# First edge of each receiver block: a one-hot row pick on TensorE in place of an indirect row gather, with the own products moved into block 0

## The reference, cut to what matters

```python
h = node_features @ W + b_W;  xi, xj = split(h, 2)
xji = xj[senders] + (edge_features @ W_e + b_We)
xji = xji / (in_degree[receivers][..., None] + 1e-06)
nodes = xi + segment_sum(xji, receivers)             # layer 0
x = layernorm(x + nodes)
h = x @ W;  norm = dinv[src] * dinv[dst]             # layer 1, with self loops
out = segment_sum(h[src] * norm[:, None], dst) + b   # then batch norm, leaky relu
x = layernorm(x + leaky(batchnorm(out)))
```

## Time and profile before

| what | before |
|---|---|
| median of 3 runs | 942.07 us |
| runs | 942.12, 940.08, 942.07 us |
| span of the profiled execution, all that is given of its own time | 940.7 us |
| busy in the span: TensorE (PE), VectorE (DVE), ScalarE (ACT), GpSimd (POOL) | 890.2, 695.5, 454.9, 419.3 us |
| bytes moved | 244.8 MB |

### The profile page before, as it was taken

How to read it: one execution, slowest core, us unless ns; L and a number is a source line. 1 busy time by engine, 2 the same in 40 slices (tenths; PEclk the granted TensorE clock), 3 DMA queues, 4 the chain that set the end, 5 groups by cost and what they waited for, 6 DMA issues and landing times.

```text
span 940.7 us, 30861 instructions
## 1 busy us (share of the span) xinstructions
PE 890.2 (95%) x12193; PEld 794.2 (84%) x12193; DVE 695.5 (74%) x1636; ACT 454.9 (48%) x962; POOL 419.3 (45%) x498
## 2 busy tenths in 40 slices
PE   5679999999999999999999999999999999999995
PEld 4667888888988998989999999999988888888864
DVE  5898999999999998898888899888842111112255
ACT  3765665566656665565565556565542000000035
POOL 3347557555764555655565575544332011111100
PEclk9689999999999999999999999999999999999998
DMA  5475888899797987777687777688767887779635
GB/s 164 132 232 212 314 289 293 313 325 315 263 324 286 316 304 236 266 218 248 244 284 249 236 250 211 243 281 258 231 207 305 341 346 285 270 259 324 248 123 165
DMA packets 95727, 244.82 MB, mean 260 GB/s; under 512 B 41194, under 2 KB 63400, under 8 KB 89688
## 3 DMA queue, kind: packets, MB, share of 16 engines
q1 hardware_dynamic: 92312, 237.49, 72.5%
q0 software_dynamic: 2400, 4.88, 1.6%
q10 hardware_dynamic: 864, 0.39, 0.2%
HBM read 183.88 MB, written 58.85 MB: 258 GB/s over the span
## 4 chain that ended last, share of the span: by engine, by line
PE 81%; DVE 10%; issue 3%; ACT 2%; DMA 2%; POOL 0%; ACTq 0%; DVEq 0%
PE x_ps L846 24%; PE pair_ps L911 17%; PE pair_ps L828 13%; PE e_ps L865 10%; PE x_ps L854 9%; DVE key_oh L597 3%; DVE lo_oh L594 3%; PE j_ps L893 2%; DMA early_in<-sums_z 1%; PE pair_ps L920 1%; PE j_ps L894 1%; PE u_vps L1379 1%; ACT counts L1035 1%; DMA xsplit<-in_dst 1%; PE j_ps L943 1%
## 5 line engine op out<-in xcount | busy, mean ns | idle before, releaser
L1035 ACT CAST counts<-pair_ps 128x784 bf16<-128x784 f32 x391 | 315.4, 817 | 256.1 <-PE pair_ps L828 255.3
L846 PE MATMUL x_ps<-counts,xsplit 128*128 128x256 bf16 (+1 forms) x2450 | 306.1, 271 | 1.2 <-issue 1.2
L594 DVE TENSOR_TENSOR lo_oh<-counter,lo_t 128x1024 bf16<-128x1024 bf16 x391 | 274.4, 702 | 41.7 <-PE pair_ps L828 39.8
L846 PEld LDWEIGHTS x_ps<-counts,xsplit 128*128 128x128 f16 x2450 | 221.1, 98 | 31.4 <-issue 9.8
L597 DVE TENSOR_TENSOR key_oh<-counter,key_t 128x800 bf16<-128x800 bf16 x391 | 232.7, 595 | 0.0
L828 PE MATMUL pair_ps<-key_oh,lo_oh 128*128 128x100 bf16 x3128 | 208.5, 209 | 12.9 <-DVE key_oh L597 7.2
L828 PEld LDWEIGHTS pair_ps<-key_oh,lo_oh 128*128 128x128 bf16 x3128 | 182.9, 98 | 27.9 <-DVE key_oh L597 10.9
L865 PE MATMUL e_ps<-streams 128*32 128x128 f32 x3528 | 106.6, 274 | 0.0
L854 PE MATMUL x_ps<-counts,zown 128*128 128x256 bf16 (+1 forms) x840 | 105.9, 269 | 0.6 <-issue 0.6
L911 PE MATMUL pair_ps<-streams,zown 128*128 128x256 bf16 x878 | 99.0, 273 | 0.0
L865 PEld LDWEIGHTS e_ps<-streams 128*32 128x32 f32 x3528 | 93.4, 110 | 4.8 <-issue 1.0
(11 more groups left out here) (179 smaller groups left out, 881.1 us busy)
## 6 DMA issues: line engine op xcount, KB each, us to landing
streams<-in_edge_attr SPq DMA_DIRECT2D x196, 576.0 KB
counts_kept<-counts SPq DMA_DIRECT2D x10, 1600.0 KB, 9.2
streams<-counts_kept SPq DMA_DIRECT2D x6, 1600.0 KB, 6.5
counts<-counts_kept SPq DMA_DIRECT2D x4, 1600.0 KB, 6.5
counts_kept<-counts SPq DMA_DIRECT2D x2, 3136.0 KB, 12.1
streams<-counts_kept SPq DMA_DIRECT2D x2, 3136.0 KB, 14.6
edst<-in_dst SPq DMA_DIRECT2D x196, 4.5 KB, 1.9
counts<-in_x SPq DMA_DIRECT2D x3, 1024.0 KB, 8.9
```

The costliest lines, as they stand in the source:

```text
L594: dv.tensor_tensor(lo_oh[:, at % RING, :, :, :], counter[:, :, :].unsqueeze(1).to_broadcast([P, SW // 2, P, 2]), pairs(lo_t[b % 2][:, w]). ...
L846: last = nc.tensor.matmul(x_ps[:, 0, 0:n], xsplit[:, q // 2, q % 2, :], by_hi[:, q // 2, :], start=(q == 0), stop=(q == 2 * HS - 1))
L1035: a.copy(out.rearrange("p h (g n) -> p h g n", g=2), pair_ps[at % 2][:, :, 0:4 * KW].rearrange("p g (n h) -> p h g n", h=HI)[:, 0:HS]).the ...
```

## The change

The heads and the row gathers are gone. For each block SP (ScalarE's queue for blocks 1 to 3) loads 128 consecutive rows of `dst`, one a partition, with the next row's head as a 126th word (`load_rows`; four buffers, and one buffer with two loads for the last two blocks). ScalarE makes them float and subtracts the block's first receiver (`float_rows`). VectorE compares the row's head and the next row's head with each pair's threshold, in two operations (`find_below`, `pick_rows`), which gives a one-hot matrix of 128 rows by 128 pairs. TensorE multiplies that by the rows (`find_rows`), so that each pair gets its row, and VectorE counts in it (`count_row`, `start_of`), from PSUM. GpSimd has no part in it any more. For blocks 4 to 24 the steps for block b + 3 stand in block b: `float_rows` in slot 0 on ScalarE, `find_below` in slot 1 and `pick_rows` in slot 2 on VectorE, `find_rows` in slot 3 on TensorE, `count_row` in slot 8.

All 13 own products stand in slots 0 to 12 of block 0, each with the next piece's transposition behind it, in one PSUM buffer. x is loaded into the upper part of `streams`, where block 0's second group of edges comes later, so that group's load and its one-hots wait for the split of x. The reductions `largest` move into slots 0, 2 and 4 of block 0, `split_high` to slots 13 to 15 of block 0, `split_low` to slot 15 and to slots 2 and 4 of block 1. The far heads and their three spreads fall away.

```diff
-HIGH_AT, LOW_AT, HEADS_AT = (4, 6, 9), (7, 10, 13), (9, 11, 13)
+LARGEST_AT = (0, 2, 4)
+TOP_AT, SCALES_AT, SPREAD_AT = 5, 8, 12
+HIGH_AT, LOW_AT = (13, 14, 15), (15, 18, 20)
...
+        def load_rows(engine, b):
+            reach(engine, S["rows_float"], b - ROW_RING + 1)
+            engine.dma_start(rows_i[b % ROW_RING][:, :],
+                             bass.AP(tensor=dst.tensor, offset=first_row(b) * HR, ap=[[HR, P], [1, HR + 1]]))\
+                  .then_inc(rows_in[b % ROW_RING], 16)
...
             def load_edges(b, g, starts):
                 reach(sp, S["e_summed"], edge_group(b - 1, g) + 1)
+                if b == 0 and g == 1:
+                    sp.wait_ge(S["x_low"], len(X_PIECES))
+                    sp.wait_ge(S["x_turned"], len(OWN))
...
             for b in range(NB + 2):
                 u = b - 2
+                if b + ROW_RING < LATE:
+                    load_rows(sp, b + ROW_RING)
+                if b + ROW_RING == LATE:
+                    load_late_rows(sp)
...
-            def row_of(b):
-                pool.wait_ge(S["heads_counted"], b + 1)
...
-                gather(rows[b % 2][:, :], flat_dst, row_i[:, b:b + 1], row_in[b % 2])
...
-            def count_heads(b):
...
+            def find_below(b):
+                dve.wait_ge(S["rows_float"], b + 1)
+                reach(dve, S["picked"], b)
+                dv.tensor_scalar(below[:, :], even[:, :], rows[b % 2][:, 0:1], None, ALU.is_gt).then_inc(S["below"], 1)
+
+            def pick_rows(b):
+                dve.wait_ge(S["below"], b + 1)
+                reach(dve, S["found"], b - 1)
+                dv.scalar_tensor_tensor(out=pick[b % 2][:, :], in0=even[:, :], scalar=rows[b % 2][:, HR:HR + 1],
+                                        in1=below[:, :], op0=ALU.is_le, op1=ALU.mult).then_inc(S["picked"], 1)
...
-                    if s == 1 and b + 3 < NB:
-                        count_heads(b + 3)
+                    if s == 1 and 1 <= b < NB - 3:
+                        find_below(b + 3)
+                    if s == 2 and 1 <= b < NB - 3:
+                        pick_rows(b + 3)
                     if s == 2 and b + 1 < NB:
                         make_keys(b + 1)
...
+            def find_rows(b):
+                pe.wait_ge(S["picked"], b + 1)
+                if b >= 4:
+                    pe.wait_ge(S["tabled"], b - 2)
+                    pe.wait_ge(S["starts_known"], b)
+                nc.tensor.matmul(row_ps(b), pick[b % 2][:, :], rows[b % 2][:, :], start=True, stop=True)\
+                  .then_inc(S["found"], 1)
...
+                        if s < len(OWN):
+                            own_product(s)
+                        if s + 1 < len(OWN):
+                            turn_x(s + 1)
...
+                    if s == 3 and 1 <= b < NB - 3:
+                        find_rows(b + 3)
                     if s == 3 and b + 1 < NB:
                         turn_keys(b + 1)
-                    if b == 1 and s in HEADS_AT:
-                        spread_far_heads(HEADS_AT.index(s))
...
+            def float_rows(b):
+                if b < LATE:
+                    act.wait_ge(rows_in[b % ROW_RING], 16 * (b // ROW_RING + 1))
+                else:
+                    act.wait_ge(S["late_rows_in"], 32)
+                reach(act, S["found"], b - 1)
+                a.activation(rows[b % 2][:, 0:HR + 1], (rows_i[b % ROW_RING] if b < LATE else late_rows_i)[:, :],
+                             ACT.Identity, bias=shift[:, b:b + 1]).then_inc(S["rows_float"], 1)
...
                     if b < NB and s < slots(b):
                         pair_out(b, s)
...
+                    if s == 0 and 1 <= b < NB - 3:
+                        float_rows(b + 3)
```

More of the change, by code:

```diff
@@ L44 @@
 R = E // HR
-HEAD_SPAN, HEAD_MARGIN = 98, 16
+ROW_MARGIN = 31
+ROW_RING = 4
 PER = 7
@@ L108, in edge_group, with first_row @@
     return 2 * b + g
[L111 to L119, removed]
+def first_row(b):
+    return max(0, min(b * BN * E // (N * HR) - ROW_MARGIN, R - P))
+LATE = min(b for b in range(NB) if first_row(b) == R - P)
+assert all(first_row(b) + P < R for b in range(LATE))
 def early(k):
@@ L495, in check_edges @@
                 pool.sem_inc(S["e_checked"], 1)
-            for b in range(2):
-                row_of(b)
             windows(0)
-            row_of(2)
             windows(1)
             pad_degrees(0)
-            row_of(3)
             shares(0)
             for b in range(NB):
-                if 1 <= b < NB - 3:
-                    row_of(b + 3)
                 if b + 1 < NB:
@@ L702, in z_low @@
                 last.then_inc(S["z_low"], 1)
-            dve.wait_ge(S["heads_in"], 16)
-            dv.tensor_copy(heads[:, :], heads_i[:, :]).then_inc(S["heads_float"], 1)
             dve.wait_ge(S["consts"], 4)
-            dv.tensor_copy(th[:, :], th_i[:, :])
-            dv.tensor_copy(iota[:, :], iota_i[:, :])
-            dv.memset(total[:, :], 0.0)
-            step(dv.tensor_copy(ebase[:, :], ebase_i[:, :]))
-            dve.wait_ge(S["heads_broadcast"], 1)
-            step(dv.tensor_copy(heads_sb[:, 0:NEAR], heads_ps))
-            for b in range(3):
-                count_heads(b)
+            dv.tensor_copy(shift[:, :], shift_i[:, :]).then_inc(S["rows_ready"], 1)
+            step(dv.tensor_copy(iota[:, :], iota_i[:, :]))
+            dv.tensor_scalar(even[:, :], iota[:, :], 2.0, None, ALU.mult)
+            for i in range(2):
+                dv.tensor_copy(rows[i][:, HR + 1:HR + 2], base_i[:, :])
+            step(dv.tensor_copy(th[:, :], th_i[:, :]))
+            for b in range(2):
+                find_below(b)
+                pick_rows(b)
             step(dv.tensor_copy(counter[:, :, :], iota[:, :].unsqueeze(2).to_broadcast([P, P, 2])))
-            ready_own_weights()
-            largest(0)
-            largest(1)
             for b in range(2):
@@ L721, in _ @@
                 start_of(b)
-            largest(2)
+                find_below(b + 2)
+                pick_rows(b + 2)
+            dve.wait_ge(S["consts"], CONSTS)
+            dv.memset(total[:, :], 0.0)
+            step(dv.tensor_copy(ebase[:, :], ebase_i[:, :]))
+            for b in range(2, 4):
+                count_row(b)
+                start_of(b)
+            ready_own_weights()
             make_keys(0)
```

212 lines of the change are left out of this document (91 added, 121 removed).

## The result

The changed kernel takes **1040.31 us** (median of 6 runs, 1037.51 to 1045.77), the kernel before 942.1 beside it: a ratio of **1.1035 [1.1005, 1.1066]**. The forecast was 1029, with a range of 995 to 1055. The profiled execution has a span of 1038.4 us, so 97.7 of span were lost.

The account below looks back on a forecast made before the run. TensorE was taken to bound the steady blocks, with VectorE's lead as what the change touches. Span 940.7 - 1 (start) + 70 (stall) + 18 (clock) = 1027.7 us, plus 1.4 to the median: 1029 us, range 995 to 1055.

Parts of the forecast that it names:

- The mechanism: Slot 1, blocks 2 to 21: `find_below` waits for `float_rows` behind ScalarE's copy of slot 0; VectorE's lead goes, 3.5 us a block.
- some 4: Sign of being right: VectorE idle some 4 us ahead of `find_below` in each block from 2 to 21.
- some 65 us and more: Sign of being right: TensorE idle ahead of its counts of slots 3 and 4, some 65 us and more in all.
- The stall, +70: Blocks 2 to 21: TensorE waits for late one-hots, 20 blocks by 3.5 us, +70 us, ends 64 and 78.
- `find_rows`, costed at 0: TensorE's added product, 0.27 us a block, 5.4 us over 20 blocks if nothing hid it; taken as 0.
- The start, -1: Start to end of block 1: slot 0 starts 9 us sooner, largely given back; -1 us, ends -9 and +8.
- its end of +8: Upper end of the start's term: TensorE at half clock through the own products, or block 0's second edge group late.
- The clock, +18: Blocks 2 to 21: the new waits lower TensorE's clock in two blocks of three, 1.4 us each; ends 0 and 28.
- The rival whose time came nearest, 1039: Stall and clock fall in every block: 1038 plus 1.4, so 1039 us, up to 1055; chance 0.22.
- the lower ends: Low end of the rival with the stall but a clock that holds: 1011 us, down to 1000; chance 0.17.
- the upper ones: High end of the rival with stall and clock fall in every block: 1039 us, up to 1055; chance 0.22.
- Faster: Rival: the ring of four buffers covers the wait, decided in slot 1 of each block; 933 us, chance 0.07.

Follow-up runs that it names:

- e1: Against the changed kernel, `float_rows` issued in slot 10, one block sooner, work and data unchanged: 954.19 us, ratio 1.0117.
- e2: Against the kernel before, one wait added on VectorE in slot 1 of blocks 2 to 21 for ScalarE's copy of slot 0: 1013.67 us, ratio 1.0764.
- e4: Against e1, on SP the load of block 0's second group of edges stands behind the store of block 0's counts: 950.43 us, ratio 1.008.
- e6: Against e4, rows and one-hot in bf16 instead of f32 for the product that finds the row: 949.2 us.
- e10: Against a 952.39 us kernel with early splits of x, VectorE's halves moved from slots 6, 8, 10 of block 0 to 10, 12, 14: 940.5 us.
- e5: Against e4, start reordered: two reductions ahead of the first keys, last third of x loaded later, splits in slots 9 to 15 of block 0: 950.32 us.
- e9: Against e5 and e6 together (948.92 us), splits of x in block 0 moved to slots 5 to 10, last third of x still loaded later: 952.39 us.
- e3: Against the changed kernel, `float_rows` stands in front of ScalarE's copies of slot 0 instead of behind them: 1014.48 us, ratio 1.0776.

## Why the prediction was right, and which terms were off

**The mechanism was right.** The idle time ahead of `find_below` came as forecast (4.74 us in block 14; "some 4"), TensorE's waits for the one-hots were 69.0 us ("some 65 us and more"), the blocks without `float_rows` lost nothing, and e1 and e2 show it from both sides: the same work without the wait gives back 86 us, the wait without the work takes 71.5.

**The stall, +70: under by some 10.** In block 14 the waits are 0.38, 1.63 and 1.19, where I had 2.1 and 1.3: 3.2 together, near the 3.4. But the block lost 4.0 and not 3.6, because VectorE came later still. Slot 4's one-hots end 10.59 us behind TensorE's start of slot 0 (478.85 + 0.70 - 468.96), where I had 10.29 (413.65 - 403.36), and the count takes them up 0.06 later. (The waits are less than the loss, since `find_rows` took 0.29 of the last one and since the products before each of the three run on for some 0.16 us after the point where the next count would have begun: 3.2 + 0.3 + 0.5.) From `find_below` up to there VectorE doesn't stand idle once, so the 0.3 are durations taken too small: 0.48 from the start of `float_rows` to that of `find_below`, where I had 0.27, and small differences in VectorE's work of slots 2 to 4. The other 0.14 of the 0.5 a block is that I had put the early blocks at 3.3.

`find_rows`, costed at 0 because it would "fall into the wait that follows", did so: its 0.29 (477.06 - 476.77) stands ahead of slot 4's wait, which is ended by VectorE. It costs its 0.28 a block only where that wait is gone, as e4's late blocks (28.19 against 27.89) and e6 show. Which side of the last wait an instruction stands on decides.

**The start, -1: off by 7, just inside its end of +8.** The changed kernel is behind by 6.0 at block 1's mark. VectorE's first one-hots, ScalarE's `float_rows` of block 1 and VectorE's last one-hots of slot 4 of block 1:

```profile
19.89 0.69 DVE L601 TENSOR_TENSOR lo_oh<-counter,lo_t 128x1024 bf16<-128x1024 bf16 x1 [2.32 <-ACT lo_t L1066]
...
61.95 0.42 ACT L1126 ACTIVATE rows<-rows_i,shift 128x126 f32<-128x126 int32 x1
...
71.27 0.61 DVE L604 TENSOR_TENSOR key_oh<-counter,key_t 128x800 bf16<-128x800 bf16 x1
```

The first one-hots began at 19.89 and not at 17, mainly since the first window gather took 7.48 us in the chain. `float_rows` ended at 62.37 where I had 57.8: those 2.9 us, and most of the rest in slots 6 to 12, which took 17.8 us (35.5 to 53.3) where I had 16. From there on it went as forecast: slot 4's one-hots were ready 9.5 us later, where I had 9.4. The clock at its lower level, which the term had at its upper end, did come from 60 to 75 us, but VectorE's one-hots ended TensorE's waits there; what it cost was not separated.

Past the term's end block 2 lost another 4.8, against the 4.0 of a late block. Where no stall of `find_below` covers it, the wait for the store is worth 4.5 us (a lag of 6.6 in e1, 2.1 in e4); here 0.8 of it shows. I had noted that the load of the second group of edges waits for the last split, and asked who needs those edges, not what stands behind that load in SP's queue.

**The clock, +18: over.** By the marks, blocks 3 to 21 lost 98.5 - 10.8 = 87.7 us; 19 of 4.0 would be 76. Of the other 11.7, 8.5 lie in blocks 3 to 8, where the clock was 0.87 to 0.97; 1.4 are the end of block 21's stall, behind its mark, and 1.8 are spread over blocks 9 to 21, where it was 1.00. With a stall of 4.0 in each block, 8.5 us are then the most that the clock cost, and not all of them are its own: between the marks of blocks 2 and 3, up to 116.00 us, ScalarE waited 5.2 us for what the profile puts down to another core or an unknown queue, and TensorE 1.8 us for ScalarE; and e1, without the stall, lost 1.8 us there too. What the rest is made of was not separated. From 300 us on it was 1.00 with waits of 1.6 to 1.75 and 1.2 to 1.3 in every block, about those of the earlier trace rows, where it had fallen. I had taken the length of the waits as what decides. What a late block has beside it is more work between two counts: ten products of 128x256 in 1.25 us, where block 1 has seven in 0.94; that this is the reason was not tested. The rival whose time came nearest, 1039, supposed a fall in every block: right sum, wrong reason. The rule of the Trainium skill that I named for it ("TensorE: Matmul & The Clock Gate", section "A second HAM failure mode: psum-queue depth-cycling") agrees with the early blocks of this trace (0.87 to 0.97) and not with the late ones (1.00).

**The sum.** Forecast -1 + 70 + 18 = 87 of span; measured by the marks 6.0 (to block 1) + 0.8 (block 2 beyond a stall) + 20 x 4.0 + 11.7 = 98.5. The errors are +7 and +0.8, +10 and, for all that is left over, -6 us; that the last took off from the others is luck. Two ends among the rivals don't follow from their own terms: the lower ends give 997 where I had 1000, the upper ones 1056 where I had 1055. Neither bears on the result. "Faster" fell where it was to be decided: the ring of four doesn't cover a wait that ends 2.95 us behind TensorE's start of slot 0.

## What to carry to other kernels

Where one engine runs ahead of another through a ring of buffers, ask of each wait in its queue not whether the data is late but **at which slot its producer stands, as against the slots by which the waiting engine leads**: a wait for a step of the same slot, or of the one before it, handed the lead back in slot 1 of each block as in block 0's splits. Moving the producing step a lead or more ahead cost nothing here, and gave 86 us (e1) and 12 (e10). And follow a held queue to its end: what hurt in block 2 was not the load that waited but the store behind it.

## What the runs showed of the hardware that was not expected

- A window gather on GpSimd's queue took 7.48 us from issue to landing while x was being loaded. In the kernel before, the gather for the same keys was issued at 20.37, behind the load of x, and took 2.5 us (the 5.2 that e5's expectation gives for it are the row gather's). With a third of x loaded later (e5, e9) the keys began no sooner, but two reductions then stood in front of them on VectorE, so that the gather's own time there is not known.
- Two waits of 1.2 to 1.75 us in each block of some 32 us left the granted clock at 1.00 from 300 us on, while it was 0.87 to 0.97 in the early blocks.
- A 128x127 product in f32 takes TensorE 0.28 us to the next instruction, in bf16 0.06.
- Four of the 14 traces, the changed kernel's, e3's, e6's and e10's, hold one place where ScalarE and VectorE both stand idle and start again at the same moment, at 116.00, 283.62, 594.81 and 588.58 us: ScalarE's idle time before it is 5.2 to 6.5 us, VectorE's 2.0 to 2.7, and the profile puts both down to another core or an unknown queue. One core runs the kernel; the cause stays open.
